# Splitting the first x tile by halves of its rows, in four PSUM banks, at the start of an attention and FFN kernel

## What is computed

```python
k = x @ W_lat + b_lat                       # 512 x 128 per batch
q = (x @ W_d + b_d).reshape(Bx, Tx, NH, L)  # 16 heads of 128
att = jnp.einsum('bhtl,bsl->bhts', q, k) * scale
att = jnp.where(causal, att, -jnp.inf)
y = jnp.einsum('bhts,bsl->bhtl', softmax(att), k)
out = y.reshape(Bx, Tx, NH * L) @ W_proj + b_proj
```

## Time and profile before

| what | us |
|---|---|
| median of 3 runs | 280.67 |
| the profiled execution | 280.85 |
| its span, first to last instruction | 279.1 |
| TensorE busy in it | 271.7 (97%) |
| VectorE, ScalarE, GpSimd busy | 218.8, 212.3, 154.2 |

### The profile page before, as it was taken

How to read it: one execution, slowest core, us unless ns; L and a number is a source line. 1 busy time by engine, 2 the same in 40 slices (tenths; PEclk the granted TensorE clock), 3 DMA queues, 4 the chain that set the end, 5 groups by cost and what they waited for, 6 DMA issues and landing times.

```text
span 279.1 us, 6206 instructions
## 1 busy us (share of the span) xinstructions
PE 271.7 (97%) x1885; PEld 247.0 (89%) x1885; DVE 218.8 (78%) x701; ACT 212.3 (76%) x578; POOL 154.2 (55%) x214
## 2 busy tenths in 40 slices
PE   8999999999999999999999999999999999999991
PEld 4878999999999998999999999999999999999990
DVE  2698777777777777788789888899988887779882
ACT  3689877777787778887787877787777778879471
POOL 5458444444433336555666866665657847238652
PEclk9999999999999999999999999999999999999997
DMA  5594110111101111111111111110112200020151
GB/s 178 144 293 124 39 40 28 30 36 38 34 25 35 38 39 38 40 38 42 38 38 40 38 40 38 39 37 22 38 39 79 78 21 21 1 76 2 58 171 38
DMA packets 18842, 15.53 MB, mean 56 GB/s; under 512 B 1641, under 2 KB 18178, under 8 KB 18818
## 3 DMA queue, kind: packets, MB, share of 16 engines
q1 hardware_dynamic: 18242, 13.65, 16.4%
q0 software_dynamic: 576, 1.58, 1.6%
HBM read 12.60 MB, written 2.63 MB: 55 GB/s over the span
## 4 chain that ended last, share of the span: by engine, by line
PE 97%; DVE 0%; POOLq 0%; issue 0%; ACT 0%; DVEq 0%
PE bank L412 21%; PE bank L414 20%; PE bank L413 20%; PE bank L547 9%; PE ps_out L412 7%; PE ps_out L413 6%; PE ps_out L414 6%; PE bank L527 3%; PE bank L637 3%; PE bank L470 1%; PE bank L424 1%; POOLq L60 0%; PE bank L676 0%; PE bank L678 0%; PE bank L557 0%
## 5 line engine op out<-in xcount | busy, mean ns | idle before, releaser
L841 ACT ACTIVATE probs<-probs,negmax 128x512 f32<-128x512 f32 (+3 forms) x128 | 72.6, 575 | 6.0 <-DVE negmax L1026 4.6
L1384 POOL TENSOR_TENSOR wd_hi<-wd_raw,zero 128x256 fp32r<-128x256 f32 x31 | 23.8, 768 | 87.5 <-DVE probs L1098 84.5
L849 ACT CAST pT_hi<-bank 128x512 fp32r<-128x512 f32 (+2 forms) x96 | 43.4, 488 | 27.7 <-PE bank L547 27.3
L1026 DVE CUSTOM_DVE_ANT_0 probs<-bank,mask_row 128x512 f32<-128x512 f32 (+3 forms) x128 | 59.2, 482 | 0.7 <-PE bank L504 0.7
L1035 DVE TENSOR_TENSOR pT_lo<-bank,pT_hi 128x512 fp32r<-128x512 f32 (+2 forms) x96 | 52.8, 552 | 6.0 <-ACT pT_hi L849 5.6
L547 PEld LDWEIGHTS bank<-ident_r,prob_words 128*128 128x128 f32 x310 | 33.0, 140 | 5.5 <-ACT probs L893 0.4
L412 PE MATMUL ps_out<-wp_hi,yT_hi 128*128 128x256 f32 x124 | 37.0, 299 | 0.0
L412 PE MATMUL bank<-kT_hi,qT_hi 128*128 128x256 f32 (+2 forms) x94 | 36.5, 388 | 0.0
L413 PE MATMUL ps_out<-wp_lo,yT_hi 128*128 128x256 f32 x124 | 35.0, 282 | 0.0
L414 PE MATMUL ps_out<-wp_hi,yT_lo 128*128 128x256 f32 x124 | 34.9, 282 | 0.0
L1055 DVE TENSOR_TENSOR yT_lo<-bank,yT_hi 128x512 fp32r<-128x512 f32 x31 | 21.4, 690 | 15.9 <-PE bank L414 14.1
(11 more groups left out here) (203 smaller groups left out, 732.1 us busy)
## 6 DMA issues: line engine op xcount, KB each, us to landing
wd_raw<-in_L_attn_W_d SPq DMA_DIRECT2D x32, 128.0 KB, 2.2
wp_raw<-in_L_attn_W_proj SPq DMA_DIRECT2D x32, 128.0 KB, 2.1
wf_raw<-in_L_ffn_w SPq DMA_DIRECT2D x2, 1024.0 KB, 6.7
x_nat<-in_L_attn_x SPq DMA_DIRECT2D x4, 256.0 KB, 3.4
out<-z_all SPq DMA_DIRECT2D x4, 256.0 KB, 2.3
picked<-ranked SPq DMA_DIRECT2D x2, 258.0 KB, 2.7
wlat_raw<-in_L_attn_W_lat SPq DMA_DIRECT2D x1, 128.0 KB, 3.8
bproj_all<-in_L_attn_b_proj SPq DMA_DIRECT2D x1, 128.0 KB, 3.4
```

The lines of the kernel that those rows point to most:

```text
L841: act.activation(p_tile(s, j), p_tile(s, j), ACT.Exp, bias=negmax[:, s, j:j + 1], scale=-1.0, accum_out=sums[:, s, j:j + 1]).then_inc(exp_ ...
L849: act.copy(pT_hi[:, dst], src).then_inc(pt_hi_done, 1)
L1026: dve.tensor_tensor_reduce(p_tile(s, j), score_bank[j], mask_row[:, (TILES - 1 - j) * P:], -SCALE, -MASKED, ALU.add, ALU.min, accum_out=ne ...
L1384: pool.tensor_tensor(hi, src, nothing, ALU.add).then_inc(hi_done, 1)
```

## The change

The first x tile is turned into four banks instead of two: half 0 of the rows into `ps_t0` and `ps_t1`, half 1 into `ps_s2` and `ps_s10`, 256 columns in each. `x_turned` is raised after each half and chunk, four times. ScalarE's copy and VectorE's subtraction follow in four 256-wide steps each, instead of two 512-wide ones; VectorE does the two of half 0 ahead of the high part of W_lat. An idle product of 256 columns stands between the halves on TensorE, and behind them there are one of 512 and one of 256 columns instead of two of 512. In `project_k_first` the low part of x in chunk 1 trades places with the low part of W_lat in chunk 1. The biases are turned into `ps_s3` instead of `ps_s2`. Batch 1's x is handled as before, with other semaphore counts.

```diff
+        x_banks = [[ps_t0[:, 0:KEEP], ps_t1[:, 0:KEEP]], [ps_s2[:, 0:KEEP], ps_s10[:, 0:KEEP]]]
+        def x_half(t, half, c):
+            return t[:, c, half * KEEP:(half + 1) * KEEP]
...
-        WAKING, AWAKE = 6, 2
+        WAKING, BETWEEN, AWAKE = 6, (2,), (4, 2)
...
-                        dst = (ps_t0, ps_t1)[c]
+                        dst = (ps_t0, ps_t1)[c][:, half * KEEP:(half + 1) * KEEP] if b else x_banks[half][c]
...
-                        if half:
+                        if half or not b:
                             last.then_inc(x_turned, 1)
+                    if not b and half == 0:
+                        keep_awake(BETWEEN)
...
+                term(w_hi, x_hi, 0, first=True)
+                pe.wait_ge(x_hi_done, 4)
+                term(w_hi, x_hi, 1)
+                pe.wait_ge(x_split, 3)
+                term(w_hi, x_lo, 0)
                 pe.wait_ge(wlat_split, 1)
+                term(w_lo, x_hi, 0)
+                pe.wait_ge(x_split, 4)
+                term(w_hi, x_lo, 1)
                 pe.wait_ge(bias_in, 48)
...
+                term(w_lo, x_hi, 1, last=True).then_inc(kT_ready, 1)
...
+            def x_high_halves():
+                for half in range(2):
+                    for c in range(CH):
+                        act.wait_ge(x_turned, CH * half + c + 1)
+                        act.copy(x_half(xT_hi[0], half, c), x_banks[half][c]).then_inc(x_hi_done, 1)
...
+            x_low_half(0, 0)
+            x_low_half(0, 1)
             dve.wait_ge(wlat_in, 16)
             dve.tensor_copy(wlat_hi[:], wlat_raw[:]).then_inc(wlat_hi_done, 1)
             for c in range(CH):
-                x_low(0, c)
+                x_low_half(1, c)
```

More of the change, by code:

```diff
@@ L419, in turn_x @@
                     for c in range(CH):
-                        dst = (ps_t0, ps_t1)[c]
+                        dst = (ps_t0, ps_t1)[c][:, half * KEEP:(half + 1) * KEEP] if b else x_banks[half][c]
                         if b and half == 0:
                             pe.wait_ge(x_split, c + 1)
-                        for j in range(2 * half, 2 * half + 2):
+                        for j in range(2):
                             last = pe.transpose(dst[:, j * P:(j + 1) * P].bitcast(F32R),
-                                                x_words[:, b * TILES + j, c * P:(c + 1) * P], ident_r[:, :])
@@ L426, in turn_x, with term @@
-                        if half:
+                                                x_words[:, b * TILES + 2 * half + j, c * P:(c + 1) * P], ident_r[:, :])
+                        if half or not b:
                             last.then_inc(x_turned, 1)
+                    if not b and half == 0:
+                        keep_awake(BETWEEN)
             def project_k_first():
                 w_hi, w_lo, x_hi, x_lo = wlat_hi, wlat_lo, xT_hi[0], xT_lo[0]
+                def term(w, x, c, first=False, last=False):
+                    return pe.matmul(ps_kT, w[:, c, :], x[:, c, :], start=first, stop=last, skip_group_check=True)
@@ L432, in project_k_first @@
                 pe.wait_ge(wlat_hi_done, 1)
[L433 to L438, removed]
+                pe.wait_ge(x_hi_done, 3)
@@ L439, in project_k_first @@
+                term(w_hi, x_hi, 0, first=True)
[3 more added lines that the diff above has]
+                term(w_hi, x_lo, 0)
                 pe.wait_ge(wlat_split, 1)
-                for c in range(CH):
-                    pe.matmul(ps_kT, w_lo[:, c, :], x_hi[:, c, :], start=False, stop=False, skip_group_check=True)
+                term(w_lo, x_hi, 0)
+                pe.wait_ge(x_split, 4)
+                term(w_hi, x_lo, 1)
@@ L442, in project_k_first @@
                 pe.wait_ge(bias_in, 48)
[L443 to L446, removed]
+                pe.transpose(ps_s3[:, 0:BIASES], bias_rows[:, :], ident[0:BIASES, 0:BIASES]).then_inc(bias_turned, 1)
+                term(w_lo, x_hi, 1, last=True).then_inc(kT_ready, 1)
@@ L464, in turn_k, with keep_awake @@
                 last.then_inc(k_turned, 1)
-            def keep_awake(times):
-                for _ in range(times):
-                    pe.matmul(ps_s3[:, :], still[:, :], still[:, :].unsqueeze(1).broadcast_to([P, TILES, P]),
+            def keep_awake(sizes):
+                for n in sizes:
+                    pe.matmul(ps_s3[:, 0:n * P], still[:, :], still[:, :].unsqueeze(1).broadcast_to([P, n, P]),
                               start=True, stop=True)
             pe.wait_ge(still_filled, 1)
-            keep_awake(WAKING)
+            keep_awake((TILES,) * WAKING)
             pe.wait_ge(ident_r_done, 1)
@@ L542, in turn @@
                 if at.fixed == 1 and n < CH:
-                    pe.wait_ge(x_split, CH + n + 1)
+                    pe.wait_ge(x_split, 2 * CH + n + 1)
                 a = 0
@@ L798, in split_queries, with x_high_second @@
                                scale=1.0).then_inc(q_hi_done, 1)
-            def x_high(b):
+            def x_high_halves():
[3 more added lines that the diff above has]
+                        act.copy(x_half(xT_hi[0], half, c), x_banks[half][c]).then_inc(x_hi_done, 1)
+            def x_high_second():
                 for c in range(CH):
-                    act.wait_ge(x_turned, CH * b + c + 1)
-                    act.copy(xT_hi[b][:, c, :], (ps_t0, ps_t1)[c][:, :]).then_inc(x_hi_done, 1)
+                    act.wait_ge(x_turned, 2 * CH + c + 1)
+                    act.copy(xT_hi[1][:, c, :], (ps_t0, ps_t1)[c][:, :]).then_inc(x_hi_done, 1)
             def kT_high(b):
@@ L826, in k_high @@
                 act.copy(k_hi[b][:, :, :], ps_ks[b][:, 0:SEQ - P].rearrange("p (j l) -> p j l", l=LAT)).then_inc(k_hi_done, 1)
-            x_high(0)
+            x_high_halves()
             act.wait_ge(wd_in[0], 16)
@@ L834, in _ @@
             kT_bias(0)
-            x_high(1)
+            x_high_second()
             def exps(at, js):
@@ L988, in _, with x_low_half, x_low_second @@
             dve.memset(still[:, :], 0.0).then_inc(still_filled, 1)
[L990 to L993, removed]
+            def x_low_half(half, c):
+                dve.wait_ge(x_hi_done, CH * half + c + 1)
+                dve.tensor_tensor(x_half(xT_lo[0], half, c), x_banks[half][c],
+                                  x_half(xT_hi[0], half, c).bitcast(F32), ALU.subtract).then_inc(x_split, 1)
+            def x_low_second(c):
+                dve.wait_ge(x_hi_done, 2 * CH + c + 1)
+                dve.tensor_tensor(xT_lo[1][:, c, :], (ps_t0, ps_t1)[c][:, :],
+                                  xT_hi[1][:, c, :].bitcast(F32), ALU.subtract).then_inc(x_split, 1)
             def kT_low(b):
@@ L1069, in period @@
                     if at.fixed == 0:
-                        x_low(1, 0)
-                        x_low(1, 1)
+                        x_low_second(0)
+                        x_low_second(1)
                     wait(dve, scores_ready, p * 3 + 3)
```

4 lines of the change are left out of this document (2 added, 2 removed).

## The result

The changed kernel takes 281.06 us in the median (280.80 to 281.48), against 280.65 us (280.53 to 281.17) for the kernel before, run beside it. The ratio is 1.0014 with a 95% interval of 1.0008 to 1.0020: 0.41 us slower. That is inside the 0.2% that the prediction counted as no change, but its interval leaves no change out, and 281.06 lies just beyond the predicted range. The profiled execution after took 281.06 us too, with a span of 279.3.

The account below looks back on a forecast made before the run. The prediction took TensorE, busy 97% of the span, to bound the kernel. Its terms summed to 0.00 on the profiled 280.85, which is 0.18 above the median, giving 280.67 us, range 280.3 to 281.05.

Parts of the forecast that it names:

- its sum of 0.00: Lead-in on TensorE: 0.01 gained at the third product of k, lost again at the fourth, so no net change.
- Three more instructions per engine at most lie in idle time: Instructions the change adds on each engine: claimed to fall in idle time and counted as no cost.
- The last sentence of the prediction's list of signs: Sign of being wrong: queries near 7.97 and yet another total, meaning a reason outside the lead-in.
- Third and fourth product, the bias transpose: Lead-in on TensorE: third product at 6.63, fourth held to 6.90 by GpSimd's W_lat low part, transpose staying at 7.46.
- the 0.38: Delay of the queries' start around the biases' transpose, put on the transpose itself, not on a wait for x.
- the first rival: The 0.38 is a wait for x, or x lands later when timed; earlier halves then pay: 280.1 to 280.5; chance 0.14.
- Not delayed, with 0.06 to spare: VectorE's cast of W_lat: the two subtractions ahead end by 5.56, before the load lets it start at 5.62.
- the rival's smaller case: VectorE's new order delays W_lat's cast: W_lat landing 0.3 earlier when timed costs about 0.1; whole rival's chance 0.07.
- I keep the rise where it is: Clock's rise from 1.2 to 2.4 GHz stays within the first product of k; a later rise had chance 0.09.
- The Trainium skill's rule that the prediction cited: Clock's rise varies by some 500 ns between runs; either kernel could lose up to two products, 0.4.
- Its upper bound of 281.05: Top of the range, to take in most of VectorE's order and a clock late by one or two products.
- the second half's transposes: TensorE's transposes of x's half 1: move back by 0.15, ending their pairs at 4.68 and 4.94, cost 0.

Follow-up runs that it names:

- b_act2: Kernel before plus two one-column copies on ScalarE at the start, written into an existing tile: 280.88 us, ratio 1.0006.
- b_dve2: Kernel before plus two one-column fills on VectorE at the start, written into an existing tile: 280.74 us, ratio 0.9995.
- b_both: Kernel before plus two one-column copies on ScalarE and two one-column fills on VectorE, written into an existing tile: 280.95 us, ratio 1.0007.
- b_again: Kernel before, unchanged, measured and profiled once more: 280.71 us, ratio 0.9999.
- a_move: Kernel after plus four one-column copies on ScalarE and three one-column fills on VectorE, written into an existing tile: 280.76 us, ratio 1.0003.
- a_again: Kernel after, unchanged, measured and profiled once more: 281.00 us, ratio 1.0009 against the kernel before.
- a_cast_space: Kernel after with four ScalarE and three VectorE fillers, W_lat's cast ahead of x's subtractions, 64 empty bytes ahead of FFN tiles: 280.58 us, ratio 0.9993.

## Why the prediction was wrong

The lead-in, to which the prediction gave all its working, came out as its sum of 0.00 said. The total did not.

- **The step that failed** is "Three more instructions per engine at most lie in idle time", costed at nothing. Two of them on ScalarE and two on VectorE do lie in idle time, and their own durations cost nothing. But they move what stands behind them in each engine's list against two pauses of about 0.4. The runs put 0.2 to 0.27 on TensorE's path for ScalarE's and 0.07 to 0.17 for VectorE's; in the medians 0.22 (`b_act2`), 0.05 (`b_dve2`) and 0.29 for both (`b_both`). No row of the lead-in could have shown it: the places are at 29 and 127 us, and no row was read there. The last sentence of the prediction's list of signs had the case: queries as expected "and yet another total, a reason outside the lead-in".
- **What the pauses are** is shown in part. That they depend on the count of instructions ahead is shown by the table. The traces also record reads of instructions, packets of 8 KB and of the kind `instruction` on DMA queue 14, and these move with the counts. Such a read begins 0.64 to 0.67 after the start of ScalarE's copy in the five kernels with 63 records ahead, 1.08 to 1.11 after it in the five with 61, and 2.52 to 2.56 before it in the three with 67. For VectorE's subtraction it is 0.75 to 0.95 after with 407, 1.15 to 1.51 after with 405, and 0.24 to 0.51 before with 410. The packets don't name an engine; which one they serve is read from whose count moves them. That speaks for pauses at places where the engine goes on to a new piece of its code. But they are not a wait for a read that the trace records: in the execution after, none is under way from 26.8 to 30.2, nor from 116.3 to 128.7. What the engine does in the pause stays open. The Trainium skill, "Runtime: NRT & Kernel Launch", section "Instruction fetch mechanics", says that an engine's instructions stream in by blocks, fetched ahead by the sequencer's own DMA queue, and that crossing into a new block costs little because it is mostly hidden. A place bound to the count, with a read that follows it, agrees with that; "hidden" doesn't, where the pause falls on work that others wait for: 0.38 on ScalarE and 0.36 on VectorE.
- **Third and fourth product, the bias transpose.** After and `b_again` agree to 0.01 from the first product to the queries (1.99 and 2.00). The fourth product waited for GpSimd's low part of W_lat as forecast: 0.29 idle on its weight load, that part ending at 6.57 (5.83 plus 0.74). From the fifth product to the queries, with the transpose between, it is 0.83 after and was 0.84 in the earlier trace rows, although the last low part of x was there at 6.42 (5.67 plus 0.75). So the 0.38 belongs to the transpose, as the prediction chose, and not to a wait for x. That half of the first rival is out.
- **"Not delayed, with 0.06 to spare"** held in every profile of the new order, with less to spare. W_lat's cast started at 5.62 in the earlier trace rows because the load landed at 5.59; in the other executions the load landed at 5.12 to 5.46. With the new order the cast starts at 5.33 to 5.46, 0.02 or 0.03 behind its load (landed at 5.30 to 5.43), as it does in `b_again` (5.43 behind 5.41). In the execution after it was close: the second subtraction started at 5.13, and such steps follow each other 0.33 apart, so VectorE would not have been free before 5.46 either. Had W_lat landed at 5.12, as in `b_both`, the order would have held the cast, which is the rival's smaller case (W_lat landing 0.3 earlier, about 0.1); no profile of the new order caught it. `a_move` ends 0.10 above before, within its interval of nothing, and what that is stays open.
- **"I keep the rise where it is"** did not hold. In the execution after, the idle products of 4.95 (one of 512 columns, one of 256) start 0.22 apart, against 0.44 for 512 columns in the earlier trace rows, so the clock had risen before them; in the kernel before with two instructions more it hadn't for the first two products of k. TensorE's rows of `b_act2`:

```profile
4.95 1.08 PE L470 MATMUL bank<-still 128*128 128x512 bf16 x2
5.66 0.80 PE L434 MATMUL ps_out<-xT_hi,wlat_hi 128*128 128x512 f32 x1
6.26 0.63 PE L436 MATMUL ps_out<-xT_hi,wlat_hi 128*128 128x512 f32 x1
6.68 0.55 PE L438 MATMUL ps_out<-xT_lo,wlat_hi 128*128 128x512 f32 x1
...
8.13 0.40 PE L412 MATMUL bank<-xT_hi,wd_hi 128*128 128x512 f32 x1
```

  The first product of k starts 0.30 ahead of the earlier trace rows and the queries 0.16 behind. The record of the full granted clock begins at 7.01 here, and over all executions anywhere from 3.92 (`a_again`) to 7.01, and in `a_cast_space` at 10.35. The point of the rise moves from execution to execution in both kernels, which, with W_lat's landing, spreads the start of the queries from 7.67 to 8.16, and once to 9.38. It isn't the cause of the difference: kernels of either lead-in have early and late ones (4.64 to 7.01 with the old one, 3.92 to 6.20 with the new), and the stretches of the table start behind it. The Trainium skill's rule that the prediction cited is borne out in kind; the spread seen here is larger than its 500 ns.

In the terms of the sum: lead-in 0.00 predicted, 0.01 measured against `b_again`; the added instructions 0 predicted, 0.34 measured against `b_again` (0.25 and 0.09), 0.24 to 0.29 by the medians of `a_move` and `b_both`. By the medians some 0.1 of the 0.41 is not accounted for.

Two slips in the prediction's arithmetic had no part in this. Its upper bound of 281.05 was to take in a clock late by two products, but at its own price of 0.21 each that is 281.09. And the second half's transposes, moved back by 0.15 from 4.57 and 4.82, end their pairs at 4.72 and 4.97, not 4.68 and 4.94.

## What to carry to other kernels

When a change adds or drops a few instructions on a busy engine, don't only ask where they lie: everything behind them in that engine's list shifts against the places where the engine pauses, and 0.1 to 0.3 us can come or go far from the edit. When a small difference doesn't show up where the edit is, line up the two traces by differences between the same products and look for the first place where they part; then test with idle instructions that write into a tile that exists already. A filler that brings a tile of its own moves the tiles behind it, and here that alone was worth more than the effect in question.

## What was not expected of the hardware

- Pauses of some 0.36 to 0.42 us stand at fixed counts in an engine's list: with 63 records ahead on ScalarE and 407 on VectorE; two fewer, or three to four more, and the same instruction runs without one. A read of 8 KB of instructions begins 0.64 to 0.95 after the paused instruction's start, and none is under way in the pause.
- 64 bytes of empty space per partition ahead of the FFN tiles change the pace of the last float32r products of 256 columns from 0.119 to 0.113 us and the kernel from 280.69 to 280.25.
- The clock's rise was seen anywhere from 3.92 to 7.01 us, and once at 10.35, in executions whose first idle product starts at 1.05. The latest went with an execution in which TensorE had waited for x.
